# A graph layer on one core: a third PSUM buffer in the edge stage, sums taken later, more directly gathered groups, and a reordered head

## The reference

```python
h  = maximum(layernorm(x), 0)
m  = concat([h[src], 0, edge_attr]) @ W1 + b1          # per edge, 256 wide
m  = relu(batchnorm(m, g1, be1))                        # statistics over all edges
agg = segment_sum(m, dst) / maximum(count(dst), 1)      # per node
h2 = concat([h, 0, agg]) @ W2 + b2                      # 385 wide
h2 = relu(batchnorm(h2, g2, be2))                       # statistics over all nodes
out = x + relu(h2 @ W3 + b3)
```

## Time and profile before

| what | value |
|---|---|
| median of three runs | 3299.74 us |
| the profiled execution, its own time | 3334.19 us |
| its span, first to last instruction | 3332.4 us |
| TensorE busy, mean granted clock | 2238.2 us (67%), 0.792 |
| VectorE busy | 1809.5 us (54%) |
| GpSimd busy | 1771.4 us (53%) |
| ScalarE busy | 966.0 us (29%) |
| DMA | 742.39 MB, 223 GB/s in the mean |

### The profile page before, as it was taken

One profiled execution on the slowest core, in us unless ns is written; L12 is line 12 of the kernel. 1 busy time (PEld: TensorE's weight loads), 2 busy tenths in 40 slices (PEclk: granted clock), 3 DMA queues, 4 the chain that ended last, 5 costly groups with the idle time before them and its releaser, 6 DMA issues.

```text
span 3332.4 us, 42140 instructions
## 1 busy us (share of the span) xinstructions
PE 2238.2 (67%) x14721; PEld 1041.0 (31%) x14721; DVE 1809.5 (54%) x5080; ACT 966.0 (29%) x1574; POOL 1771.4 (53%) x1874
## 2 busy tenths in 40 slices
PE   1644665656566656656565655666656899999998
PEld 1522222222232222223222222222222444444448
DVE  2644444444353544444444444444544888888977
ACT  1411212212121212112212121221211555565546
POOL 7065666666666666666666656666665222222222
PEclk6866777777676777777777676767776899999999
DMA  7455666656666665666666655666665999999964
GB/s 187 163 169 178 200 205 199 216 189 204 201 208 201 206 204 198 198 205 211 200 206 201 197 199 193 206 208 202 212 194 178 338 343 340 341 341 343 344 234 148
DMA packets 259989, 742.39 MB, mean 223 GB/s; under 512 B 46395, under 2 KB 86165, under 8 KB 259774
## 3 DMA queue, kind: packets, MB, share of 16 engines
q1 hardware_dynamic: 176238, 518.88, 42.9%
q0 software_dynamic: 80672, 219.91, 23.0%
q10 hardware_dynamic: 2864, 0.86, 0.1%
HBM read 502.68 MB, written 236.81 MB: 222 GB/s over the span
## 4 chain that ended last, share of the span: by engine, by line
PE 37%; another core or an unknown queue 26%; DVE 17%; issue 15%; DMA 4%; ACT 1%; POOL 0%; DVEq 0%; SPq 0%; POOLq 0%; ACTq 0%
PE psum L1169 9%; DVE late L902 7%; PE psum L1146 6%; PE psum L1268 6%; PE psum L1287 6%; DVE late L903 5%; DMA late<-m_d 3%; PE psum L1181 2%; PE psum L1298 2%; PE psum L1351 2%; DVE sums L939 2%; PE psum L1229 1%; PE psum L1173 1%; DVE late L980 1%
## 5 line engine op out<-in xcount | busy, mean ns | idle before, releaser
L537 POOL DMA_INDIRECT sums<-P_d,late x1597 | 1514.7, 948 | 958.6 <-issue 450.4
L939 DVE TENSOR_TENSOR sums<-psum,sums 128x1024 f32<-128x1024 f32 (+1 forms) x400 | 487.8, 1219 | 1167.0 <-remote 834.6
L631 ACT ACTIVATE sums<-sums 128x1024 f32<-128x1024 f32 x416 | 438.7, 1055 | 1815.5 <-DVE sums L939 973.4
L1181 PE MATMUL psum<-late 128*98 128x128 bf16 x1661 | 225.4, 273 | 831.9 <-DVE late L903 589.2
L1169 PE MATMUL psum<-late,sums 64*128 64x256 f32 x3320 | 661.3, 496 | 115.6 <-issue 86.7
L1169 PEld LDWEIGHTS psum<-late,sums 64*128 64x128 f32 x3320 | 377.1, 233 | 647.2 <-issue 567.4
L1146 PE MATMUL psum<-sums,ones 128*32 128x512 f32 x830 | 578.7, 788 | 0.3 <-ACT sums L631 0.3
L1147 PE MATMUL psum<-sums,ones 128*32 128x512 f32 x830 | 578.5, 788 | 0.0
L1148 PE MATMUL psum<-sums,ones 128*32 128x512 f32 x830 | 578.4, 787 | 0.0
L1149 PE MATMUL psum<-sums,ones 128*32 128x512 f32 x830 | 578.2, 787 | 0.0
L980 DVE TENSOR_TENSOR late<-late,psum 128x1024 f32<-128x1024 f32 x416 | 492.4, 1211 | 38.8 <-DMA late<-m_d 34.9
(11 more groups left out here) (196 smaller groups left out, 1977.4 us busy)
## 6 DMA issues: line engine op xcount, KB each, us to landing
m_d<-sums SPq DMA_DIRECT2D x415, 512.0 KB
late<-m_d SPq DMA_DIRECT2D x415, 512.0 KB, 5.4
sums<-in_ea_main SPq DMA_DIRECT2D x103, 512.0 KB
sums<-P_d,late POOLq DMA_INDIRECT x1597
P_d<-sums SPq DMA_DIRECT2D x24, 512.0 KB, 2.9
nodes<-in_x SPq DMA_DIRECT2D x24, 256.0 KB
late<-in_x SPq DMA_DIRECT2D x24, 256.0 KB, 3.0
out<-late POOLq DMA_DIRECT2D x24, 256.0 KB, 3.4
```

Source lines behind the costliest of these rows:

```text
L537: pool.indirect_dma_start(out=m_s[s][0:r, k * L:(k + 1) * L], out_offset=None, in_=P1_d, in_offset=bass.IndirectOffsetOnAxis(ap=idx[0:r, G ...
L939: dve.tensor_tensor(m_s[s][0:r, 0:w], ps_m[g % 2][0:r, 0:w], m_s[s][0:r, 0:w], ALU.add).then_inc(s_m, 1)
L1181: ins = pe.matmul(ps_cnt[0:NH, 0:P], hot_hi[0:r, g % 2, k, 0:NH], hot_lo[0:r, g % 2, k, :], start=(g == 0 and k == 0), stop=(g == NG - 1), ...
```

## The change

- PSUM: `ps_m` gets a third buffer (banks 6 and 7). TensorE's product of g waits for the entry three before it in a ring of products and of direct groups' transposes, instead of for the addition of g-2.
- TensorE's order in a step becomes: product of g, counts of g-2, sums of g-3. The one-hots get three slots.
- Direct groups: `X_GROUPS` 20, statistics at g-8, scaling at g-7, transposes at g-2, copy at g-4 of ScalarE's loop. The range computation's scratch (1,920 columns) is laid over the first direct slots and so is loaded and used late: load at step 91, computation from 94, transpose at 98, send at 100, windows at 105.
- Head: four transpose buffers (banks 6, 7, 4, 5), the product three blocks behind the transposes, ScalarE's copy two behind; statistics one chunk further ahead; `node_bias` and `split_destinations` after block 12.
- Tail: SyncE stores `out` instead of GpSimd; the first block's relu in two halves; VectorE's aggregation before the odd column's work; the odd row's copy inside the branch.

```diff
-X_GROUPS = 18
+X_GROUPS = 20
+LEAD = 3
+TURN_SLOTS = 4
+HOT_SLOTS = 3
...
-        xg_n = min(len(free), X_GROUPS, GF // 8)
+        xg_n = min(len(free), X_GROUPS, GF // 12)
...
-        ps_m = [psum[:, 2 * i:2 * i + 2, :].rearrange("p a b -> p (a b)") for i in range(2)]
+        ps_m = [psum[:, i:i + 2, :].rearrange("p a b -> p (a b)") for i in (0, 2, 6)]
+        ps_turn = [psum[:, i, :] for i in (6, 7, 4, 5)]
...
+                if g == LOAD:
+                    sp.wait_ge(s_clear, 1)
+                    load_ranges()
...
-            for b in range(NB):
-                pool.wait_ge(s_o, b + 1)
-                row_tiles_dma(pool, out, o_n[b % NODE_SLOTS], b, False, s_out[b % NODE_SLOTS])
...
-                if g >= 2:
-                    dve.wait_ge(s_cnt, g - 1)
+                if g >= HOT_SLOTS:
+                    dve.wait_ge(s_cnt, g - HOT_SLOTS + 1)
...
             for b in range(NB):
                 turn(b)
-                if b >= 1:
-                    table(b - 1)
-            table(NB - 1)
+                if b >= 3:
+                    table(b - 3)
+            for b in range(max(0, NB - 3), NB):
+                table(b)
...
+            def buffer_free(entry):
+
+                if ring_of[entry] >= LEAD:
+                    gathered, i = ring[ring_of[entry] - LEAD]
+                    pe.wait_ge(s_xTs if gathered else s_m, i + 1)
...
-                if g >= 2:
-                    pe.wait_ge(s_m, g - 1)
+                if g + 2 in xg_no:
+                    turn_gathered(xg_no[g + 2])
+                buffer_free((False, g))
+                if g == TURN + 1:
+                    pe.wait_ge(s_rngs, 1)
...
-                if g >= 1:
-                    stats(g - 1)
-                if g + 1 in xg_no:
-                    j, buf = xg_no[g + 1], ps_m[(g + 1) % 2]
-                    pe.wait_ge(s_xh, j + 1)
-                    pe.wait_ge(s_m, g + 2 - 2)
-                    for k in range(GT):
-                        ins = pe.transpose(buf[:, k * P:(k + 1) * P], xg[j][:, k, :], ident[:, :])
-                    ins.then_inc(s_xT, 1)
+                if g >= 2:
+                    counts(g - 2)
+                if g >= 3:
+                    stats(g - 3)
```

More of the change, by code:

```diff
@@ L244, in build @@
         xg_no = {g: j for j, g in enumerate(xg_at)}
+        scratch = taken[0]
+        grp = early(GC * EB)
+        grp_f = grp[:, 0:GC * EB].rearrange("p (c e) -> p c e", c=GC)
+        grp_i = grp[:, 0:GC * EB].bitcast(I32).rearrange("p (c e) -> p c e", c=GC)
+        grp_end, taken[0] = taken[0], scratch
+        base_bc = early(GC * P)
+        win_bc = early(NS)
+        rng_row = early(2 * GC * P, 1)
+        win_row = early(3 * NS + 4 + 2 * NB, 1)
+        assert max(taken[0], grp_end) <= scratch + (XG_OVER + 1) * GE
+        CLEAR = xg_at[min(XG_OVER, xg_n - 1)] + 1
+        LOAD, RANGE = CLEAR + 2, CLEAR + 5
+        ring = []
+        for g in range(NG):
+            if g + 2 in xg_no:
+                ring.append((True, xg_no[g + 2]))
+            ring.append((False, g))
+        ring_of = {entry: n for n, entry in enumerate(ring)}
+        place_m = {g: ring_of[False, g] % LEAD for g in range(NG)}
+        place_T = [ring_of[True, j] % LEAD for j in range(xg_n)]
+        TURN = next(g for g in range(RANGE + 2, NG) if place_m[g + 1] == LEAD - 1
+                    and not any(h in xg_no for h in range(g - 2, g + 6)))
+        SEND, BACK = TURN + 2, TURN + 7
+        assert BACK < GF
         rng = sb("rng", [P, 2 * GC])
@@ L485, in _ @@
             sp.wait_ge(s_n1s, KC * NB)
+            for b in range(min(NODE_SLOTS, NB)):
+                row_tiles_dma(sp, x, x_n[b], b, True, s_xn[b])
             for b in range(NB):
                 i = b % NODE_SLOTS
-                if b >= NODE_SLOTS:
-                    sp.wait_ge(s_o, b - NODE_SLOTS + 1)
-                row_tiles_dma(sp, x, x_n[i], b, True, s_xn[i])
+                sp.wait_ge(s_o, b + 1)
+                row_tiles_dma(sp, out, o_n[i], b, False, s_out[i])
+                if b + NODE_SLOTS < NB:
+                    row_tiles_dma(sp, x, x_n[i], b + NODE_SLOTS, True, s_xn[i])
+            for b in range(max(0, NB - NODE_SLOTS), NB):
+                sp.wait_ge(s_out[b % NODE_SLOTS], slot_count(b, row_parts, NODE_SLOTS))
         @block.gpsimd
@@ L619, in _ @@
                 h_rows(b)
-                if b >= 1:
-                    hT_copy(b - 1)
-                if b % XL == XL - 1 and c + 2 < NXL:
-                    ln_sqrt(c + 2)
-            hT_copy(NB - 1)
+                if b >= 2:
+                    hT_copy(b - 2)
+                if b == 0 and NXL > 2:
+                    ln_sqrt(2)
+                if b % XL == XL - 1 and c + 3 < NXL:
+                    ln_sqrt(c + 3)
+            for b in range(NB - 2, NB):
+                hT_copy(b)
             for g in range(NG):
@@ L825, in _ @@
             ln_scale(0)
-            for c in range(1, min(4, NXL)):
+            for c in range(1, min(5, NXL)):
                 ln_stats(c)
@@ L835, in _ @@
                 if b % XL == XL - 1:
-                    if c + 2 < NXL:
-                        ln_scale(c + 2)
-                    if c + 4 < NXL:
-                        ln_stats(c + 4)
-                elif c >= 1 and beside:
+                    if c + 3 < NXL:
+                        ln_scale(c + 3)
+                    if c + 5 < NXL:
+                        ln_stats(c + 5)
+                elif c >= 6 and beside:
                     beside.pop(0)()
@@ L1000, in statistics, with aggregate @@
                 dve.bn_stats(bn2_st[:, c, b, :], n1_rows(c, b)).then_inc(s_bst, 1)
+            def aggregate():
+                dve.wait_ge(s_bst, KC * NB)
+                for c in range(KC):
+                    dve.bn_aggr(bn2_mv[:, c, :], bn2_st[:, c, :, :].rearrange("p b s -> p (b s)"))
             with dve.If_eq(flag, 0):
@@ L1153, in stats, with counts, turn_gathered @@
                 ins.then_inc(s_st, 1)
+            def counts(g):
+                pe.wait_ge(s_hot, g + 1)
+                r = rows(g)
+                for k in range(tiles(g)):
+                    ins = pe.matmul(ps_cnt[0:NH, 0:P], hot_hi[0:r, g % HOT_SLOTS, k, 0:NH], hot_lo[0:r, g % HOT_SLOTS, k, :],
+                                    start=(g == 0 and k == 0), stop=(g == NG - 1), skip_group_check=True)
+                ins.then_inc(s_cnt, 1)
+            def buffer_free(entry):
+                if ring_of[entry] >= LEAD:
+                    gathered, i = ring[ring_of[entry] - LEAD]
+                    pe.wait_ge(s_xTs if gathered else s_m, i + 1)
+            def turn_gathered(j):
+                buffer_free((True, j))
+                pe.wait_ge(s_xh, j + 1)
+                for k in range(GT):
+                    ins = pe.transpose(ps_m[place_T[j]][:, k * P:(k + 1) * P], xg[j][:, k, :], ident[:, :])
+                ins.then_inc(s_xT, 1)
             pe.wait_ge(s_hTs, NB)
```

117 lines of the change are left out of this document (57 added, 60 removed).

## The result

The changed kernel took 3279.57 us in the median of 6 runs (3264.99 to 3287.20), the kernel before 3305.85 us (6 runs, 3295.94 to 3312.94): a ratio of 0.9919, 95% interval [0.9899, 0.9938]. That is faster by 26 us where 186 were forecast. 3279.57 lies inside the range of 3035 to 3285, but far from 3114. One plain fact is needed to read what follows: two chips ran the kernel before in 2869 and 2871 us, and several findings hold on one kind of chip only. Where it takes about 3300 us, I call the chip "of the slow kind".

What follows compares the result with a forecast made beforehand. The edge stage was taken as bound by a rhythm of GpSimd's gathers and stops, with TensorE's completions late. Terms -164 - 20 + 0 + 0 + 3 - 5 = -186 us against 3299.74 gave 3114 us, range 3035 to 3285.

Steps and rivals of the forecast that it cites:

- TensorE's completions reach the others late: Edge stage: while GpSimd issues gathers without a pause, TensorE's completion signals arrive late; VectorE waits 834.6 us in 165 waits.
- They come through when GpSimd stops: Edge stage: late completions arrive in a bunch about when GpSimd stops for lack of a free slot; 173 stops of 2.48 us.
- with three buffers it is three groups, 2.3 x 1.6 = 3.7: Edge stage: GpSimd's run between stops grows from 2.3 to 3.7 groups, 107 stops instead of 173; -164 us, ends -131 and -216.
- the sums stay tied to the addition: Edge stage: sums of g still follow the addition of g, so slots are held only behind one more product.
- 16 x 1.25 = -20: Four more direct groups: sixteen P1 gathers of 1.25 us leave the edge stage, -20 us, and return as x gathers in the head.
- 0, ends -10 and +20: Head: gathers last 20 us longer, but each bunch lets two blocks through, eight done by 116 us; no net change.
- wrong would be a first P1 gather after 190 us: Head: a sign against the forecast, which put the first P1 gather between 157 and 187 us.
- Ranges: Range computation at steps 91 to 105: loads and small VectorE steps covered by seven slots; 0 us, ends -10 and +10.
- End of the edge stage and tail: Two terms: more sums and counts after the last addition, +3 us; shorter chain around the W3 product, -5 us.
- The buffer bridges nothing: Rival for the edge stage, chance 0.14: run length stays 2.3; 3278 us, up to 3298 if the head pays 20 us.
- The rule of the Trainium skill: Cited for the no-help side: PSUM double-buffering gave no further gain in a DMA-held kernel; by it the sum would be 3278 us.
- Nearly all stops vanish: Rival for the edge stage, chance 0.07: GpSimd runs through, stage 1984 us instead of 2425, some 2860 us in all; half-way 3000.

Runs made afterwards that it cites:

- c_pause8: Changed kernel with eight small GpSimd fills, each waited for, behind every second group of P1 gathers; 3285.06 us, one run.
- b_linear: Changed kernel with each P1 gather by index replaced by a plain transfer of 128 consecutive rows, same bytes, same queue; slow-kind chip; 2179.01 us, one run.
- a_lead2: Changed kernel with two PSUM buffers in the ring instead of three, counts and sums as late as in the changed kernel; 3310.78 us, ratio 0.9955.
- a_early: Changed kernel with three PSUM buffers, but counts of g and sums of g-1 behind the product of g, as before the change; 3326.41 us, ratio 1.0006.
- a_x16: Changed kernel with 16 direct groups instead of 20; 3307.43 us, ratio 0.9945.
- a_oldhead: Changed kernel with the head order of the kernel before (two transpose buffers, product one block behind); 3284.61 us, ratio 0.9878.
- b_oldhead: Changed kernel with the head order of the kernel before, timed again on another chip of the slow kind; 3288.79 us, ratio 0.9876.
- b_head2: Changed kernel with the head's product and copy two blocks behind instead of three, on a slow-kind chip; 3286.21 us, ratio 0.9880.
- c_again: The changed kernel as it is, timed on a further chip of the slow kind; 3275.60 us, ratio 0.9930.
- b_pace: Changed kernel with a small GpSimd fill and a wait for it after every P1 gather, on a slow-kind chip; 3320.63 us, one run.
- a_head2: Changed kernel with the head's product two blocks behind instead of three, on a chip where the kernel before took 2868.75 us; 2847.82 us, ratio 0.9919.
- a_again: The changed kernel as it is, on a chip where the kernel before took 2868.75 us; 2861.48 us, ratio 0.9972.

## Why the prediction was wrong

**The bound.** "TensorE's completions reach the others late" came out right: the signals in the trace name TensorE and clear VectorE and ScalarE. "They come through when GpSimd stops" is borne out by c_pause8, with a rest of lateness left. That gathers by index bring it on is shown by b_linear, as far as scattered and consecutive rows are the same.

**The step that failed: "with three buffers it is three groups, 2.3 x 1.6 = 3.7".** It measured 2.8 in the result (143 stops), so -63 us in the place of -164, outside the term's ends of -131 and -216. And of what was gained the buffer is the smaller part: 8 to 12 us (a_lead2), the later sums 25 to 29 (a_early). Each of these is what is lost when it alone is taken away, so they need not add up to 63.

Why a deeper ring hides so little stays open. I had treated the lateness as a delay that a buffer bridges. Another reading is a budget of silence. Take the time from the first P1 gather to the end of the last, less their busy time and 0.30 us per gap. That silence is 402 us before, 386 in a_early, 377 in a_x16, 373 in a_lead2 and in a_oldhead, 377 in b_oldhead, 368 in b_head2, 344 in the changed kernel, 343 in c_again; with pauses it is 386 in b_pace and 352 in c_pause8. Pauses change it little: 352 against 343 on one chip, 386 against 368 and 377 on the other, whether it is cut into 90 stops and 1581 crumbs, some 150 stops or 208 pauses. Per group it is 0.87 to 1.01 us. The sums say just as well that TensorE gets through a group in 5.85 (c_again) to 5.99 us (before) while such gathers are issued, whatever lies ahead of it. Nothing that ran tells these two apart; a pause that makes GpSimd's own pitch longer than that was not tried on this kind of chip.

One thing in the kernel that the prediction passed over bears on it. It says that the sums stay tied to the addition, but the square that they need has three slots and waits for TensorE's sums of three groups before. The change puts those sums into the same step as the product. In the kernel before, all squares of the stage start within 0.04 us of the addition or of ScalarE's being free; in the changed kernel 122 start over 1 us after both, 675 us together. So the change gave TensorE's late signals a second place to be waited for. A fourth slot for squares was not tried.

**The other direct groups.** "16 x 1.25 = -20" came as -9 in the profile of the edge stage; with what the head pays, the whole is a gain of 0.15 to 0.26%, 5 to 9 us, if it is one (a_x16).

**The head**, "0, ends -10 and +20", was +36. Two errors. The crawl does not let two blocks through per bunch: by 106 us VectorE had added four half blocks, where six were done by 97 before, and by 116 five, two and a half blocks where eight were forecast. And I took the order for free behind it: from 106 to 203 us come 47 half blocks, 4.1 us a block where I had 3.2. With the product two behind (b_head2) 46 come from 106 to 181, 3.3 us a block. So the distance of three costs some 22 us at the first P1 gather where signals are late (180.8 against 202.3 and 203.2, on other chips), and 15 us where none is (a_head2, side by side with a_again). My "wrong would be a first P1 gather after 190 us" is what happened.

**Ranges** at 0 stand, as far as the profiles show; they were not tried by themselves. **End of the edge stage and tail** together -15 instead of +3 - 5: the stores from SyncE's queue alone gave 4.6, where I had nothing, and from the last gather to the first clip (L1014) it is 17.8 us instead of 23.1.

**The rivals.** "The buffer bridges nothing" gives 3278, as measured, but by luck: it had no gain from stops and none from later sums, and no loss in the head. The rule of the Trainium skill that I had set beside it (page "TensorE: Matmul & The Clock Gate", section "HAM oscillation — how this bites in real kernels") was nearly right in its result, since the third buffer is worth 8 to 12 us (a_lead2). Its ground was not the case here. The page tells of a kernel held up by waits for DMA, and its sentence on PSUM is about that kernel once its loop had been rearranged; where the 8 to 12 us were measured the gathers' data were there. "Nearly all stops vanish" has a slip: half of the way to 2860 us is 3080, not 3000. And the terms' ends add up to 3036 to 3182, not 3050 to 3190. Neither touches the failed step. In the sum the failed steps are: stops +101, gathers +11, head +36, tail -13 by the profiles; 186 less 135 are 51, the 52 us between the profiled spans.

## A version that beats both

b_head2, the changed kernel with the product two blocks behind: 0.9880 [0.9859, 0.9901] where the changed one has 0.9930 [0.9903, 0.9956] and 0.9919 [0.9899, 0.9938], and on the other kind of chip 0.9919 [0.9897, 0.9941] where the changed one has 0.9972 [0.9962, 0.9982]. The first of these compares different chips, each against the kernel before on its own, and its interval touches that of 0.9919; the second was timed side by side. A shorter pause every second or fourth group, and a fourth slot for squares, were not tried on the slow kind.

## What to carry to other kernels

Before a buffer is added against late signals, find out whose they are. Look for a second engine that waits for the same signal, as SyncE did here; if it starts at once, the late one is another, and every condition of the wait has to be read in the kernel. Then put deliberate pauses of the suspected length into the engine that brings the lateness on, and see whether the sum of silence stays. When an order is spread further apart, price each distance by itself; here 3 for 2 cost 15 us and more in a stretch that was thought to be bound by something else. And time a kernel on more than one chip before its profile is taken for the kernel's nature.

## What the runs showed of the hardware that I had not expected

The same kernel, before the change, took 2869 and 2871 us on two chips and 3299, 3324 and 3327 us on three. Each chip was met once, and all runs of a kernel on it agree within 0.7%; that it is the chip, and not the time at which it was used, is likely but not shown. On the first kind the gathers by index disturb nobody: TensorE's signals for products come within 0.1 us of the matmuls' end (a_again), where on the other the median is 1.6 us and the longest 24 us. VectorE's and ScalarE's recorded signals are prompt on both. Plain transfers of as many bytes from the same queue hold up nobody in the edge stage on either kind, and take GpSimd 0.54 us instead of 0.95. The gathers' data are not late: by the packets of GpSimd's queue in the trace of the kernel before, sixteen of 4 bytes close each gather, and at 1047 us, just before the stop ends, those of all 648 gathers issued are through. What differs between the kinds of chip stays open, and so does what in TensorE's path is held.
